# Pattern contexts packed densely for the output projection, loads placed around the context store, the second half's norms as three tiles and one, and the rounded gelu written by ScalarE

## The reference

```python
x = x + layernorm(attn(layernorm(x)))
x = x + layernorm(ffn(layernorm(x)))

# attn: 16 main heads (scores over 128 + 64 rope dims, values of 128), latent of 64
ctx = softmax(qf @ kf.T * 192**-0.5) @ v
main_out = ctx.reshape(s, 16 * 128) @ o_w.T
# and 16 pattern heads of 16 dims
p_ctx = softmax(pq @ pk.T * 16**-0.5) @ pv
pattern_out = p_ctx.reshape(s, 256) @ sp_o_w.T
out = gates[0] * main_out + gates[1] * pattern_out

# ffn: weights quantized to MXFP4 in blocks of 32 along K, up to 1024 and down to 256
x = gelu(x @ q_up + up_bias) @ q_dn + down_bias
```

## Time and profile before

| what | us |
|---|---|
| median of 3 runs (868.11 to 871.94) | 868.13 |
| the profiled execution itself | 870.45 |
| its span, first to last instruction | 868.7 |
| mean granted TensorE clock | 0.972 |
| slot 8 begins, about | 697 |
| `o` products of tiles 0 to 3 | 770.2 to 791.1 |
| the epilogue's first product | 792.1 |
| its last product of `down` ends | 857.3 |

### The profile page before, as it was taken

The page is one execution under the profiler, slowest core; times in us unless marked ns, Lnnn a source line. Parts: engine busy times, 40 slices in busy tenths (PEclk is TensorE's granted clock), DMA queues, the critical chain, the costliest instruction groups (busy, mean ns, idle before and its releaser), DMA issues. The chain is left out here.

```text
span 868.7 us, 12785 instructions
## 1 busy us (share of the span) xinstructions
PE 802.5 (92%) x4964; PEld 463.8 (53%) x4964; DVE 590.9 (68%) x680; ACT 398.4 (46%) x499; POOL 430.6 (50%) x255
## 2 busy tenths in 40 slices
PE   5878988999999999999999999999999997999885
PEld 5663554455555554555555545545555553468754
DVE  3745765766677576856785776677666889874646
ACT  3332444555455545554555555555545553520321
POOL 1414209654856574468439552865485543530222
PEclk9979999999999999999999999999999999899978
DMA  9479462007201620351044105300621018101001
GB/s 246 175 203 286 76 169 30 10 14 147 62 1 36 112 62 2 72 114 49 13 98 114 34 13 132 71 19 14 116 62 50 25 51 312 40 14 61 0 1 49
DMA packets 92704, 68.52 MB, mean 79 GB/s; under 512 B 61858, under 2 KB 71396, under 8 KB 92388
## 3 DMA queue, kind: packets, MB, share of 16 engines
q1 hardware_dynamic: 92644, 67.71, 30.2%
HBM read 42.02 MB, written 17.04 MB: 68 GB/s over the span
## 5 line engine op out<-in xcount | busy, mean ns | idle before, releaser
L966 POOL TENSOR_TENSOR acc<-acc,em 128x1024 f32<-128x1024 f32 x96 | 237.2, 2470 | 96.5 <-ACT em L1024 96.4
L1117 DVE TENSOR_REDUCE m2p<-xb 128x2 f32<-128x1024 f32 x128 | 155.2, 1220 | 77.5 <-PE xb L1281 77.1
L1125 DVE TENSOR_REDUCE m<-xb 128x2 f32<-128x1024 f32 x128 | 155.7, 1219 | 63.1 <-PE xb L1281 63.0
L1015 ACT ACTIVATE ep<-xb 128x1024 f32<-128x1024 f32 x128 | 131.1, 1024 | 111.7 <-PE xb L1281 111.7
L1024 ACT ACTIVATE em<-xb 128x1024 f32<-128x1024 f32 x128 | 131.1, 1024 | 102.0 <-PE xb L1281 92.5
L1316 PE MATMUL pvm<-em,cpair 128*64 128x512 f32 x512 | 138.3, 618 | 7.4 <-ACT ctxr L1070 7.4
L929 POOL TENSOR_TENSOR rot<-rot,sin 128x512 f32<-128x512 f32 x32 | 40.9, 1278 | 116.2 <-DMA rot<-raw 116.2
L1281 PEld LDWEIGHTS xb<-pq,pk 49*128 49x128 f32 x256 | 23.9, 184 | 101.0 <-issue 81.3
L966 POOL TENSOR_TENSOR acc<-em 128x1024 f32<-128x1024 f32 x16 | 38.1, 2378 | 64.7 <-PE xb L1424 50.9
L1327 PE MATMUL pvp<-ep,vp 128*32 128x512 f32 x512 | 69.1, 612 | 0.0
L1281 PE MATMUL xb<-pq,pk 49*128 49x512 f32 x256 | 64.3, 499 | 0.0
(11 more groups left out here) (282 smaller groups left out, 1297.3 us busy)
## 6 DMA issues: line engine op xcount, KB each, us to landing
rot<-raw SPq DMA_DIRECT2D x128, 64.0 KB, 2.0
pk<-spqk_d SPq DMA_DIRECT2D x48, 128.0 KB, 4.3
sums<-rec_d SPq DMA_DIRECT2D x32, 128.0 KB, 2.9
ctx_d<-ctxr SPq DMA_DIRECT2D x14, 256.0 KB, 2.0
pq<-spqk_d SPq DMA_DIRECT2D x48, 64.0 KB, 2.3
wraw<-wst_d SPq DMA_DIRECT2D x7, 384.0 KB, 5.8
em<-in_o_w SPq DMA_DIRECT2D x1, 2048.0 KB, 7.8
vp<-vp_d SPq DMA_DIRECT2D x8, 256.0 KB, 4.8
```

Of the source, the lines that this page charges most:

```text
L966: pool.tensor_tensor(acc[:, :, :], before, em[:, j:j + 2, :], ALU.add).then_inc(added, 1)
L1015: act.activation(ep[:, j:j + 2, :], src[:, :, :], ACT.Exp, scale=PAT_SCALE).then_inc(ep_ready, 1)
L1117: dve.tensor_reduce(m2p[:, t, 2 * tp:2 * tp + 2, kt], src[:, :, :], AX, ALU.max).then_inc(x_dve, 1)
L1125: dve.tensor_reduce(m2[:, q, t, :, kt], src[:, :, :], AX, ALU.max).then_inc(x_dve, 1)
```

## The change

Pattern contexts are packed: the 16 rows of a head without the other 16, eight heads in a tile, so two products per token tile and not four. `load_patterns` brings four pieces of 16 rows per pair from DRAM, `move_pattern` moves patterns 6 and 7 from `prec` to their place by four DMAs each, and both divisions now write `prec`. The next pattern's sums may be spread to `prec` only when pattern 6 has left it (`pat_back`). `sp_o_w` is loaded in whole rows, without the two memsets, and one transposing job goes.

`load_epilogue` is taken apart. `vo`, `ffn` and patterns 0 to 4 are loaded in slot 7, behind the waits at which `load_late` stood and ahead of the gather of that slot; main contexts of pairs 0 to 2 in slot 8 ahead of the store; pattern 5 and pairs 3 to 5 behind it. The pattern division of slot 9 is at step 5, and the last two quantizing steps come behind it.

In the epilogue tiles 4 to 7 are normalised as three and one, the last four as two and two, and the transposes of half 1 stand between the two `down` of half 0. ScalarE evaluates gelu a second time into the rounded `hhi`, for all m of half 0 and even m of half 1, where VectorE had copied. The functions around these (`evacuated`, `wait_hi`, `final_norm`) follow: they count the new semaphores and groups.

```diff
-    if v >= NP:
+    if v > NP:
+        return 0 if s < 5 else 4
+    if v == NP:
         return 0 if (v, s) == (NP, 0) else 2 if (v, s) < (NP, 7) else 3
...
-    [("pm", 15), ("oT", 8), ("mm", 0), ("oT", 9)],
+    [("pm", 15), ("oT", 8), ("mm", 0)],
...
-                sp.wait_ge(cleared, 4)
                 for m in range(2):
-                    sp.dma_start(spo_nat[m][:, :, 0:PD], a["sp_o_w"][m * P:(m + 1) * P, :].rearrange(
-                        "p (g e) -> p g e", e=PD)).then_inc(spo_in, 16)
+                    sp.dma_start(spo_nat[m], a["sp_o_w"][m * P:(m + 1) * P, :]).then_inc(spo_in, 16)
...
                 if it:
                     sp.wait_ge(pat_ready, it)
                     sp.wait_ge(pat_stored, 16 * min(it, PDIRECT))
+                    if it == NP - 1:
+                        sp.wait_ge(pat_back[0], 64)
                 else:
...
-            def load_epilogue():
+            def load_weights_back():
 
                 for j in range(4):
                     sp.dma_start((rot if j < 2 else rc)[:, j % 2, :], d["vo"][j]).then_inc(ctx_back, 16)
-                sp.wait_ge(pat_stored, 16 * PDIRECT)
-                for n in range(PDIRECT):
-                    sp.dma_start(pattern_tile(g, n), d["pat"][n]).then_inc(ctx_back, 16)
-                x_wait(sp, NP - 1, ("M", NS - 1))
-                sp.wait_ge(ctx_stored, 16 * (DIRECT - 2))
-                for n in range(DIRECT - 2):
-                    half = half_of(n % 2)
-                    sp.dma_start(context_tile(g, n // 2)[:, half], d["ctx"][n // 2, :, half]).then_inc(ctx_back, 16)
                 sp.dma_start(g["xh"][:, 0, :].bitcast(F32), d["ffn"]).then_inc(ctx_back, 16)
+                load_late(2)
+                load_late(3)
+
+            def load_patterns(its):
+
+                for it in its:
+                    sp.wait_ge(pat_stored, 16 * (it + 1))
+                    for hh in range(4):
+                        at = 64 * (it // 2 % 2) + PD * hh
+                        sp.dma_start(pattern_tile(g, it // 4, it % 2)[at:at + PD, :],
+                                     d["pat"][it, 32 * hh:32 * hh + PD, :]).then_inc(ctx_back, 16)
+
+            def move_pattern(it):
+
+                sp.wait_ge(pat_ready, it + 1)
+                for hh in range(4):
+                    at = 64 * (it // 2 % 2) + PD * hh
+                    sp.dma_start(pattern_tile(g, it // 4, it % 2)[at:at + PD, :],
+                                 prec[32 * hh:32 * hh + PD, :]).then_inc(pat_back[it - PDIRECT], 16)
+
+            def load_contexts(pairs):
+                for pair in pairs:
+                    sp.wait_ge(ctx_stored, 16 * (2 * pair + 2))
+                    for half in range(2):
+                        sp.dma_start(context_tile(g, pair)[:, half_of(half)], d["ctx"][pair, :, half_of(half)]
+                                     ).then_inc(ctx_back, 16)
 
             def load_last():
 
                 sp.wait_ge(q_own, 2 * QUANTIZE)
-                sp.wait_ge(ctx_stored, 16 * DIRECT)
-                for n in range(DIRECT - 2, DIRECT):
-                    half = half_of(n % 2)
-                    sp.dma_start(context_tile(g, n // 2)[:, half], d["ctx"][n // 2, :, half]).then_inc(ctx_back, 16)
+                load_contexts((NP - 2,))
...
-                    load_epilogue()
+                    x_wait(sp, NP - 1, ("M", NS - 1))
+                    load_contexts(range(3))
                 if 2 <= v <= NP:
                     sp.wait_ge(ctx_ready, 2 * (v - 2) + 2)
                     sp.dma_start(d["ctx"][v - 2, :, HALF:S], ctxr[:, :]).then_inc(ctx_stored, 16)
...
-                    load_late(2)
-                    load_late(3)
+                    load_weights_back()
+                    load_patterns(range(5))
+                if v == NP:
+                    load_patterns((5,))
+                    load_contexts(range(3, NP - 2))
                 if 1 <= v <= NP:
                     gather(2 * (v - 1))
                     spread(2 * (v - 1))
                 if v == NP:
                     load_last()
+                    move_pattern(NP - 2)
+                if v == NP + 1:
+                    move_pattern(NP - 1)
...
-            pool.memset(ctxr[:, :], 0.0).then_inc(cleared, 1)
-            pool.memset(sums[:, :], 0.0).then_inc(cleared, 1)
...
             def pattern_division(it):
 
                 dve.wait_ge(prec_in, 64 * (it + 1))
-                to = prec[:, :]
-                if it >= PDIRECT:
-                    to = pattern_tile(g, it)
-
-                    for t in turned:
-                        dve.wait_ge(t, 128 * NP)
-                dve.tensor_tensor(to, pvr[:, :], prec[:, :], ALU.mult).then_inc(pat_ready, 1)
+                dve.tensor_tensor(prec[:, :], pvr[:, :], prec[:, :], ALU.mult).then_inc(pat_ready, 1)
 
             def between(v, s):
 
...
                         pattern_reciprocal(v - 2)
                     if s == 5:
                         main_division(2 * (v - 2) + 1)
-                    if s == 12:
+                    if s == (12 if v <= NP else 5):
...
-    for j in range(4):
-        mm = pe.matmul(out[:, HID:2 * HID], pattern_tile(g, 2 * j + half)[:, tq * P:(tq + 1) * P],
-                       g["spoT"][:, j, :], start=(j == 0), stop=(j == 3))
+    for j in range(2):
+        mm = pe.matmul(out[:, HID:2 * HID], pattern_tile(g, j, half)[:, tq * P:(tq + 1) * P],
+                       g["spoT"][:, j, :], start=(j == 0), stop=(j == 1))
     return mm
 
...
-    order = [(0, 0), (1, 0), (0, 1), (1, 1), (2, 0), (2, 1)]
+    groups = [range(0, 4), range(4, 7), range(7, 8)]
+    finals = [range(0, 4), range(4, 6), range(6, 8)]
+    order = [(0, 0), (1, 0), (0, 1), (0, 2), (1, 1), (1, 2), (2, 0), (2, 1), (2, 2)]
     jobs = [("o", t) for t in range(4, NT - 1)] + [("xT", k, 0) for k in range(NK)] + [("o", NT - 1)]
-    jobs += [("up", 0, m) for m in range(8)] + [("down", 0, m) for m in range(2)]
-    jobs += [("xT", k, 1) for k in range(NK)] + [("up", 1, m) for m in range(8)]
+    jobs += [("up", 0, m) for m in range(8)] + [("down", 0, 0)] + [("xT", k, 1) for k in range(NK)]
+    jobs += [("down", 0, 1)] + [("up", 1, m) for m in range(8)]
     jobs += [("yT", j) for j in range(2)] + [("down", 1, m) for m in range(2)]
     jobs += [("yT", 2 + j) for j in range(2)]
     index = {j: n for n, j in enumerate(jobs)}
 
-    by_act = [j[0] in ("up", "down") for j in jobs]
+    by_act = [j[0] == "down" for j in jobs]
 
     with ExitStack() as ctx:
         def sb(name, shape, dt=F32):
...
-                    pe.wait_ge(x2_ready, q + 1)
+                    pe.wait_ge(x2_ready, 1 if q == 0 else 3)
...
+        hi_by_act = [(q, m) for q in range(2) for m in range(8) if q == 0 or m % 2 == 0]
...
+            for n in range(5):
+                root(n)
             lo_of_gelu(0, 1)
-            root(2)
-            lo_of_gelu(0, 3)
-            lo_of_gelu(0, 5)
-            root(3)
-            lo_of_gelu(0, 7)
+            root(5)
+            for m in (3, 5, 7):
+                lo_of_gelu(0, m)
             for m in (1, 3, 5, 7):
                 lo_of_gelu(1, m)
-            root(4)
-            root(5)
+            for n in range(6, 9):
+                root(n)
...
-                        act.wait_ge(h_hi, t + 1)
                         act.wait_ge(h_lo[t % 2], t // 2 + 1)
-                    act.activation(hf[:, m % NHF, :], o[:, :], ACT.Gelu_apprx_tanh, bias=ub[:, m:m + 1]).then_inc(ev_act, 1)
+                    act.activation(hf[:, m % NHF, :], o[:, :], ACT.Gelu_apprx_tanh, bias=ub[:, m:m + 1]).then_inc(gelu_out, 1)
+                    if (q, m) in hi_by_act:
+                        if q and m == 0:
+
+                            act.wait_ge(pe_job, index[("down", 0, 1)] + 1)
+                        act.activation(hhi[m], o[:, :], ACT.Gelu_apprx_tanh, bias=ub[:, m:m + 1]).then_inc(h_hi[0], 1)
...
             def split_gelu(q, m):
-                n = 8 * q + m + 1
-                dve.wait_ge(ev_act, sum(by_act[:index[("up", q, m)] + 1]))
-                if q and m == 0:
-
-                    dve.wait_ge(pe_job, index[("down", 0, 1)] + 1)
-                dve.tensor_copy(hhi[m], hf[:, m % NHF, :]).then_inc(h_hi, 1)
+                if (q, m) not in hi_by_act:
+                    dve.wait_ge(gelu_out, 8 * q + m + 1)
+                    if q and m == 1:
+
+                        dve.wait_ge(pe_job, index[("down", 0, 1)] + 1)
+                    dve.tensor_copy(hhi[m], hf[:, m % NHF, :]).then_inc(h_hi[1], 1)
                 if m % 2 == 0:
-                    dve.wait_ge(h_hi, n)
...
             mix(range(4))
...
                 attention_norm(0, stage)
             for t in range(4, NT - 1):
                 mix([t])
+            attention_norm(1, 0)
             lo_of_input(0)
+            attention_norm(1, 1)
+            attention_norm(1, 2)
             mix([NT - 1])
-            for m in range(8):
-                split_gelu(0, m)
-                if m in (1, 2, 3, 5, 7):
```

(44 more changed lines are left out.)

96 lines of the change are left out of this document (54 added, 42 removed).

## The result

The changed kernel takes 854.29 us (median of 4 runs, 853.23 to 857.39) where the kernel before takes 868.66 on the same chip (median of 4). The ratio is 0.983, with a 95% interval of 0.9805 to 0.9852. The forecast was 854.3, range 849.0 to 862.0, faster.

A forecast was written before the change was run, and what follows sets the result against it. TensorE, busy 92% of the span, was taken as the bound, losing time at slot 8's end, in slot 9 and the epilogue. Terms 7.0 + 6.5 + 0.3 = 13.8 us, from the median 868.13 to 854.3; range 849.0 to 862.0.

The forecast's parts named there:

- The store: Slot 8: context store issued at 721.7 ahead of later loads; ScalarE's 9.74 us wait goes whole, copy possible at 729.8.
- Rival (e): Slot 8: six loads take twice as long, store lands after 733, cover goes; time 864 to 867; chance 0.06.
- X: End of the division of context half 14, which the first `o` product awaits: 764 against 765.8, bounds 759.3 and 768.
- Rival (b): SBUF lock between VectorE and POOL costs nothing, last pattern keeps up; block ends 780.5, time 849.8; chance 0.10.
- (a): VectorE and POOL block each other more than laid out: division ends 768, block 789, time 858.3; chance 0.17.
- TensorE's own readiness: Before slot 9's projection: TensorE free to start the first `o` product at 759.3, against 770.15 before.
- Slot 9: Four projection tiles at 4.32 instead of 5.2 us; block ends at 785.0 against 792.1, last pattern context nearly co-limiting.
- The low stretch of the clock: Slot 9: after standing about 5 us, TensorE runs at the lower clock and loses 2.7 us.
- SP in slot 7: Added loads delay the gather of sums by 4.4 us; 2 us cover, nothing lost below 0.65 us an issue.
- Slot 0: `sp_o_w` rows of 1 KB issue in about 0.5 us, one transposing job goes; gain 0.3, bounds 0 and 1.5.
- The epilogue: After the block's end: reordered norms and second gelu evaluation give 70.1 us against 76.65, 6.5 won.
- Rival (c): Epilogue's middle turns out serial, `up` of half 1 begins no sooner than before; time 860.0 or so; chance 0.12.

The follow-up runs named there:

- Experiment 1: Kernel before with one call moved: all slot 8 loads stand behind the store of the context half; 864.67 us, ratio 0.9955.
- experiment 3: Changed kernel with the last six of seven POOL adds of the last pair's second half done on 4 of 512 columns; 846.31 us, ratio 0.9738.
- experiment 2: Changed kernel with the old epilogue (norms of four tiles, gelu once, old job order); 857.31 us, ratio 0.9884.
- experiment 5: Changed kernel with the last four tiles normalised at once, as before, not as two and two; 855.03 us, ratio 0.9843.
- Experiment 6: Changed kernel with gelu evaluated once per tile, VectorE making the rounded copies; 858.05 us, ratio 0.9882.
- experiment 7: Changed kernel with eight `hf` gelu buffers in place of four; 855.81 us, ratio 0.9863.
- Experiment 8: Changed kernel with each of the 20 small pattern loads in slot 7 cut in two, 40 issues; 861.4 us, ratio 0.9922.
- Experiment 4: Changed kernel with six quantize steps of slot 8 put behind the division of half 14, pattern division one step later; 846.38 us, ratio 0.9757.
- the ninth experiment: Changed kernel with both the late quantizing steps and the last four tiles normalised at once; 845.98 us, ratio 0.9742.
- experiment 10: As the ninth experiment, with VectorE's first two low parts put into two waits for POOL's root; 846.55 us, ratio 0.9743.

## Why the prediction was right, point by point

**The store.** Right. VectorE's row of 731.18 stands at 729.38 before, so times there compare with 1.8 taken off: the store goes out at 722.2 (721.7 said), ScalarE's copy without a wait at 729.7 (729.8 said). Experiment 1 gives its price alone, 3.9 us. Rival (e) is out.

**X.** Predicted 764; measured 765.53, which is 763.7 when the 1.8 is taken off. Its two terms can be read apart from experiment 3, where one full add is left in the stretch. There the division ends at 752.43, 754.1 in the time of before. The one full add made the four steps beside it 7.07 long (from 728.46) in place of 5.00, so without any add it is 752.0; the working had 730.1 + 22.0 = 752.1. The lock's share is then 11.7 (2.07 + 9.65), and the working had 11.9. The split was another one: six adds of the seven held a step, by 1.24 to 2.20, where the working had five at 2.25 and one in part. Rival (b), a lock that costs nothing, falls with it, and so does (a). It is VectorE's queue that fixes X, and not what lies ahead: from the second mark to the first `o` product it is 75.22 us in all seven kernels that have this queue and POOL's adds as the changed one has them (itself and experiments 1, 2 and 5 to 8). TensorE's own readiness was put at 759.3; in the changed kernel, having waited 1.28 for POOL's last add, it is ready at 762.09, or 760.3 in the time of before. That 1.28 is no term of the sum, and it stayed under VectorE's wait.

**Slot 9.** Four tiles of 4.32: right. The low stretch of the clock was charged at 2.7; the first tile took 5.84 (765.79 to 771.63) in place of 4.32, so it cost 1.5: this term was mis-sized. The 1.2 us between was not won, because the block then hangs on the last pattern context, as the prediction said of it. Experiment 6, with the same code in this stage, shows it. Its first tile took 4.39, with no low stretch, and the block's end still came 20.2 us after the first product, as in experiments 2, 5 and 7, where the tile took 6.1 (20.2 to 20.5); TensorE's last wait took up the difference (2.69). In the changed kernel the reciprocal of that pattern came at X+6.8 (7.1 said), the division was done at X+16.5 (16.5), the issues at X+18.9. The product after the block waited 1.66 where 0.94 is usual, and so 0.7 us are this wait's. Block's end at X+20.9 against 21.0. Experiment 4, where X comes early and nothing waits for the pattern, shows the usual 0.95.

**SP in slot 7.** Twenty issues took 11.45, 0.57 each; the gather of sums went out at 673.90, and nothing was lost. Experiment 8 is far beyond the edge: 20.11 us for the same place in the queue is as if each issue took 1.0. An estimate of the edge: from the gather to the reciprocal it takes 2.36 there (678.61 to 680.97), which in the changed kernel would be 676.26 against a reciprocal at 677.15. So 0.9 us was left over twenty issues, and the cover would be used up near 0.62 an issue, where the prediction had 0.65.

**Slot 0: one reading was wrong.** The load of `sp_o_w` in rows of 1 KB was to issue in about 0.5 us. It did not:

```profile
65.94 6.41 SPq L730 DMA_DIRECT2D ctxr<-in_sp_o_w  x1
72.39 0.43 SPq L730 DMA_DIRECT2D sums<-in_sp_o_w  x1
```

The first issue still takes 6.41, against 6.59 in the earlier trace rows, and only the second became short (0.43, after 1.70). So the 64-byte pieces weren't what held SP at the first. What did is likely the queue itself, filled by the weight loads ahead of it; no run here took those away, and it stays open. The gain of 0.3 came all the same. The transposing job that is gone, which it was put down to, lies behind the first mark, and the last main maximum of slot 0 shows it, in the kernel before and in the changed one:

```profile
114.30 0.17 DVE L1130 TENSOR_REDUCE ms<-m 128x8 f32<-128x16 f32 x1
```

```profile
115.58 0.17 DVE L1155 TENSOR_REDUCE ms<-m 128x8 f32<-128x16 f32 x1
```

From the mark that is 11.53 us before, and 11.54 in experiment 1, which has the old slot 0. It is 11.11 to 11.14 in the changed kernel and the nine experiments that share its slot 0: 0.4 won. No run takes that job away alone. What hides it in the spans lies ahead of the mark, which came 1.7 later in the changed kernel's profile. That is no property of the change. The kernels with the same code up to there have their marks anywhere from 100.50 to 105.36, and 3.6 of the 3.9 us between the changed kernel and the ninth experiment are there before 45 us (ScalarE's copy at L340, at 44.48 and 40.93), with the wait for the first load as the largest part. Against the kernel before, 0.6 of the 1.7 is there at 92 us, and the rest comes in 16 products, the same in both, that take 4.55 us in the one and 5.61 in the other; the granted clock from 90 to 100 us is 0.83 and 0.68.

**The epilogue, in us after the block's end.** Transposes at 13.6 (13.7 said), `up` 0 at 19.2 (19.5), first low part done at 29.1 (28.8), the fifth gelu waiting for it, evaluations done at 34.3 (33.9), POOL's last low part at 35.7 (35.3). The interval of two gelus is 0.57 (0.62), although each is reported as 0.69 long. `down` 0 ends at 37.1 (36.2): this term was mis-sized. The working let it end 0.9 after POOL's last part. In fact TensorE, after its waits of 2.45 and 1.36, runs at the lower clock, 0.63 a row in place of 0.39, and is still working through the earlier products when the last part is there. Half 1 starts at 41.6 (42.3), its eight `up` take 7.3 (7.9), and the tail loses 0.4 (0.5). The epilogue is 69.2 against 70.1 said, 7.4 won and not 6.5. Rival (c), a serial middle, would have shown the start of half 1 near 47 and is out; experiment 2 has it at 45.6 with the old epilogue.

**The sum.** Said: 7.0 + 6.5 + 0.3 = 13.8. Measured between the two profiles: 7.5 + 7.4 + 0.4 = 15.3, less 2.2 given back in slots 1 to 7 and ahead of the first mark, where kernels with the same code differ by as much: 13.1. Between the medians it is 14.4. The three stages missed by +0.5, +0.9 and +0.1, all to the one side, and the 2.2 took more than that back, so the agreement to 0.1 us of the medians is luck at that size; the agreement within one us of each stage is not.

## What to carry to other kernels

Before you credit a removed stall, look at what the other engines did during it. Here VectorE used the stall to work without POOL beside it, and 6.4 us more came only when six steps, some of them held by the lock, were moved behind the one that others wait for (experiment 4). A reordering that takes one wait from TensorE in a stage where it is fed piece by piece tends to spread the wait rather than remove it (experiments 7 and 10); add up the waits behind it before you count. And compare stages from a mark close ahead of them in each execution, not from time zero, and look at several profiles before you name a cause: the start of the program alone moved by up to 5 us, and the seven slots behind it by up to 2.2, between kernels that are alike in them.

## What I had not expected of the hardware

- The issue of one DMA held SP for 6.41 us with rows of 1 KB as it had with pieces of 64 bytes (6.59). Small DMAs, on the other hand, cost 0.57 each, and 0.50 at half the size (11.45 for 20, 20.11 for 40): cutting them in two nearly doubles the price.
- VectorE's 32-wide transpose of 128x1024, with one SBUF input, took its plain 1.25 beside a POOL add, in the earlier trace rows and again at 749.69 above, while a step with two SBUF inputs went from 1.23 to 3.34.
- ScalarE starts the next 128x512 gelu 0.57 us after the one before, though each is reported at 0.69.
- The time until the first mark differs by up to 4.9 us between profiles of kernels that are alike up to there. The first wait for a load is 3.30 us in one and 0.32 in another.
- The same 16 products took 4.55 us in one profile and 5.61 in another, with the granted clock at 0.83 and 0.68 in the ten us around them.
